# A four-layer graph network on one core: the expert buffer is cleared earlier, one-hot matrices are made by ScalarE, and a step's slot sums give one signal

## What is computed

```python
# every edge part with attention; h is a projection of the nodes
score = f(h[src], h[dst])                       # one per edge and head
m = segment_max(score, dst); e = exp(score - m[dst])
out = segment_sum(e * value[src], dst) / segment_sum(e, dst)
# layer 2's experts: two of eight per node
top_p, top_idx = top_k(softmax(x @ Wr + br), 2)
y_e = gelu(xn_e @ W1[e] + b1[e]) @ W2[e] + b2[e]
x = x + sum(weight * y[top_idx])
```

## Time and profile before

| what | us |
|---|---|
| median of 3 runs | 13737.19 |
| lowest and highest | 13736.53, 13757.31 |
| the profiled execution, its own time | 13846.6 |
| its span | 13844.9 |

### The profile page before, as it was taken

How to read it: one execution, slowest core, us unless ns; L and a number is a source line. 1 busy time by engine, 2 the same in 40 slices (tenths; PEclk the granted TensorE clock), 3 DMA queues, 4 the chain that set the end, 5 groups by cost and what they waited for, 6 DMA issues and landing times. The chain is left out here.

```text
span 13844.9 us, 108219 instructions
## 1 busy us (share of the span) xinstructions
PE 7534.6 (54%) x30838; PEld 6003.5 (43%) x30838; DVE 6330.2 (46%) x16971; ACT 1340.8 (10%) x3400; POOL 6032.2 (44%) x6195
## 2 busy tenths in 40 slices
PE   3333433346665455586777564545544936666535
PEld 2333333335554345554566433333433835555423
DVE  6555654558886422232112245656522134454454
ACT  0000000000000100011122010000011200010001
POOL 1666366046664066603666406656301036666000
PEclk9999999777777655587788786777776967777767
DMA  1111111046666011202333602212523323336000
GB/s 41 53 51 54 38 54 44 13 139 172 178 178 134 13 8 8 8 14 68 92 90 90 60 13 48 47 41 44 27 26 97 109 58 93 95 94 86 19 7 16
DMA packets 454853, 872.00 MB, mean 63 GB/s; under 512 B 172059, under 2 KB 267149, under 8 KB 453907
## 3 DMA queue, kind: packets, MB, share of 16 engines
q0 software_dynamic: 277568, 621.62, 21.4%
q1 hardware_dynamic: 176714, 243.62, 6.1%
HBM read 820.84 MB, written 52.88 MB: 63 GB/s over the span
## 5 line engine op out<-in xcount | busy, mean ns | idle before, releaser
L552 POOL DMA_INDIRECT ee_rows<-e_table,net_mr_data x1000 | 993.6, 994 | 1038.7 <-POOLq L1656 469.2
L552 POOL DMA_INDIRECT ge_rows<-g_table,net_mr_data x1000 | 959.0, 959 | 674.2 <-issue 241.7
L855 POOL DMA_INDIRECT ce_rows<-c_table,net_mr_data x1000 | 947.2, 947 | 511.6 <-issue 245.5
L387 POOL DMA_INDIRECT main_slots<-em_load,em_where x784 | 809.6, 1033 | 642.5 <-DVE em_where L362 395.6
L552 POOL DMA_INDIRECT ae_rows<-a_table,net_mr_data x752 | 722.5, 961 | 592.5 <-POOLq L1656 202.4
L589 PE MATMUL ee_part_ps<-ee_message,net_eye 125*125 125x256 f32 x2000 | 607.8, 471 | 523.6 <-issue 300.8
L552 POOL DMA_INDIRECT be_rows<-b_table,b_br_data x728 | 696.2, 956 | 434.7 <-issue 172.9
L589 PE MATMUL ge_part_ps<-ge_rows,net_eye 125*125 125x256 f32 x2000 | 624.8, 481 | 304.7 <-ACT ge_part L650 210.2
L346 PE MATMUL em_look_ps<-em_table,em_hot_tT 25*128 25x125 f32 x1568 | 366.9, 421 | 739.3 <-issue 655.3
L589 PEld LDWEIGHTS ee_part_ps<-ee_message,net_eye 125*125 125x125 f32 x2000 | 472.7, 241 | 639.0 <-issue 542.4
L387 POOL DMA_INDIRECT gat_slots<-eg_load,eg_where x512 | 531.7, 1039 | 381.5 <-DVE eg_where L362 217.1
(11 more groups left out here) (1004 smaller groups left out, 16859.0 us busy)
## 6 DMA issues: line engine op xcount, KB each, us to landing
em_key_row<-main_keys SPq DMA_DIRECT2D x98, 512.0 KB
f_w<-in_L_ffn_W_dram SPq DMA_DIRECT2D x40, 1024.0 KB, 5.1
eg_key_row<-gat_keys SPq DMA_DIRECT2D x64, 512.0 KB
ce_rows<-c_table,net_mr_data POOLq DMA_INDIRECT x1000
ee_rows<-e_table,net_mr_data POOLq DMA_INDIRECT x1000
ge_rows<-g_table,net_mr_data POOLq DMA_INDIRECT x1000
main_slots<-em_load,em_where POOLq DMA_INDIRECT x784
ae_rows<-a_table,net_mr_data POOLq DMA_INDIRECT x752
```

The source lines that it names most:

```text
L387: pool.indirect_dma_start(edge["slots"], bass.IndirectOffsetOnAxis(ap=where[:, c:c + 1], axis=0), load[:, c, :], None).then_inc(scattered, 16)
L552: pool.indirect_dma_start(rows[n][:, s, :], None, table, bass.IndirectOffsetOnAxis(ap=data[:, g, s, 0:1].bitcast(I32), axis=0)).then_inc(g ...
L855: pool.indirect_dma_start(rows[:, g % RING, s, :], None, table, bass.IndirectOffsetOnAxis(ap=data[:, g, s, 0:1].bitcast(I32), axis=0)).the ...
```

## The change

1. `sorted_in`, `sorted_out` and the semaphore `cleared` are made in `program`. Between the load of X and the first sort, VectorE clears a tile of 128 x 22 x 256 words, and the sync engine issues three DMAs of 2816 rows each from it to `sorted_in` (22 KiB a partition) and one to the last 256 rows of `sorted_out`. Behind the first sort stands a block in which the sync engine waits for them. The two DMAs in `layer2_experts` go; the clearing of A stays there.
2. In the attention passes the one-hot moves from VectorE to ScalarE, as |target - ramp| and then relu(1 - that), with a drain between, first in ScalarE's order of a step, for step i+4.
3. In the attention passes the 8 slot sums give one signal, after the last. GpSimd waits for it before a step's first gather alone; ScalarE's and VectorE's waits count steps. "ce" is not changed.

```diff
@@ edge_pass, gpsimd @@
                             if kind == "mix":
                                 pool.wait_ge(message_ready, g - RING + 1)
-                            else:
-                                pool.wait_ge(slot_summed, (g - RING) * SLOTS + s + 1)
+                            elif s == 0:
+                                pool.wait_ge(slot_summed, g - RING + 1)
@@ tensor, sum_slots @@
-                        pe.matmul(part_ps[0:NP, 0:VW], const["eye"][0:NP, 0:NP], values(g)[:, s, :], start=(s == 0), stop=(s == SLOTS - 1)).then_inc(slot_summed, 1)
+                        ins = pe.matmul(part_ps[0:NP, 0:VW], const["eye"][0:NP, 0:NP], values(g)[:, s, :], start=(s == 0), stop=(s == SLOTS - 1))
+                    ins.then_inc(slot_summed, 1)
@@ scalar @@
+                def one_hot(g):
+                    if g >= HOTS:
+                        act.wait_ge(totalled, g - HOTS + 1)
+                    act.activation(hot[0:NP, g % HOTS, :], const["ramp"][0:NP, 0:2 * NP], ACT.Abs, scale=-1.0, bias=edge["rel"][0:NP, g:g + 1])
+                    act.drain()
+                    act.activation(hot[0:NP, g % HOTS, :], hot[0:NP, g % HOTS, :], ACT.Relu, scale=-1.0, bias=const["ones"][0:NP, 0:1]).then_inc(hot_ready, 1)
...
-                    act.wait_ge(slot_summed, (g + 1) * SLOTS)
+                    act.wait_ge(slot_summed, g + 1)
...
-                for i in range(-3, G + 7):
+                for i in range(-4, G + 7):
+                    if 0 <= i + 4 < G:
+                        one_hot(i + 4)
@@ vector @@
-                def one_hot(g):
-                    if g >= HOTS:
-                        dve.wait_ge(totalled, g - HOTS + 1)
-                    dve.tensor_scalar(hot[0:NP, g % HOTS, :], const["ramp"][0:NP, 0:2 * NP], edge["rel"][0:NP, g:g + 1], None, ALU.is_equal).then_inc(hot_ready, 1)
...
-                            dve.wait_ge(slot_summed, (g - 1) * SLOTS)
+                            dve.wait_ge(slot_summed, g - 1)
...
-                    if 0 <= i + 4 < G:
-                        one_hot(i + 4)
@@ routed_rows @@
-                pool.wait_ge(cleared, 32)
+                pool.wait_ge(cleared, 64)
@@ layer2_experts @@
-            @block.sync
-            def _(sp):
-                sp.dma_start(sorted_in, I["zeros256"].to_broadcast([F_ROOM + 256, D])).then_inc(cleared, 16)
-                sp.dma_start(sorted_out[F_ROOM:F_ROOM + 256, :], I["zeros256"].to_broadcast([256, D])).then_inc(cleared, 16)
@@ program @@
-        sort_edges(nc, main, I["src"], I["dst"], I["edge_attr_2"], E_MAIN, const, "em", inv_deg)
...
+        with Scope(nc, "blank") as j:
+            share = (F_ROOM + 256) // 128 // 3
+            blank, made = j.sb("blank", [128, share, D]), j.sem("made")
+            with nc.Block() as block:
+                @block.vector
+                def _(dve):
+                    dve.memset(blank[:, :, :], 0.0).then_inc(made, 1)
+
+                @block.sync
+                def _(sp):
+                    sp.wait_ge(made, 1)
+                    for n in range(3):
+                        sp.dma_start(sorted_in[n * share * 128:(n + 1) * share * 128, :].rearrange("(p a) w -> p a w", p=128), blank[:, :, :]).then_inc(cleared, 16)
+                    sp.dma_start(sorted_out[F_ROOM:F_ROOM + 256, :].rearrange("(p a) w -> p a w", p=128), blank[:, 0:2, :]).then_inc(cleared, 16)
+            sort_edges(nc, main, I["src"], I["dst"], I["edge_attr_2"], E_MAIN, const, "em", inv_deg)
+            with nc.Block() as block:
+                @block.sync
+                def _(sp):
+                    sp.wait_ge(cleared, 64)
```

More of the change, by code:

```diff
@@ L2429, in _, with layer2_experts @@
                     dve.scalar_tensor_tensor(out=X[0:NP, t, :], in0=back[0:NP, n % RING, :], scalar=share[0:NP, t, c:c + 1], in1=X[0:NP, t, :], op0=ALU.mult, op1=ALU.add).then_inc(joined, 1)
-def layer2_experts(nc, I, X, const, lower):
+def layer2_experts(nc, I, X, const, lower, sorted_in, sorted_out, cleared):
     with Scope(nc, "f") as k:
@@ L2435, in layer2_experts @@
         w1, back = k.sb("w1", [128, 2, 2, 1024]), k.sb("back", [128, 8, D])
-        sorted_in = nc.dram_tensor("f_sorted_in", (F_ROOM + 256, D), F32, kind="Internal").ap()
-        sorted_out = nc.dram_tensor("f_sorted_out", (F_ROOM + 256, D), F32, kind="Internal").ap()
-        cleared, loaded1, loaded2 = k.own_sem("cleared"), [k.own_sem(f"loaded1_{n}") for n in range(2)], k.own_sem("loaded2")
+        loaded1, loaded2 = [k.own_sem(f"loaded1_{n}") for n in range(2)], k.own_sem("loaded2")
         slot, share, tile_expert = k.sb("slot", [128, T, 2], I32), k.sb("share", [128, T, 2]), k.sb("tile_expert", [1, F_TILES], I32)
@@ L2669, in program @@
         on_vector(nc, "x_in", lambda dve: None, loads=[(X[0:NP, :, :], table_rows(I["x"]))])
-        sort_edges(nc, main, I["src"], I["dst"], I["edge_attr_2"], E_MAIN, const, "em", inv_deg)
+        sorted_in = nc.dram_tensor("f_sorted_in", (F_ROOM + 256, D), F32, kind="Internal").ap()
+        sorted_out = nc.dram_tensor("f_sorted_out", (F_ROOM + 256, D), F32, kind="Internal").ap()
+        cleared = k.own_sem("cleared")
+        with Scope(nc, "blank") as j:
[16 more added lines that the diff above has]
+                    sp.wait_ge(cleared, 64)
         sort_edges(nc, gat, I["gat_src"], I["gat_dst"], None, E_GAT, const, "eg")
@@ L2674, in program @@
                   lambda: layer1_graph(nc, I, X, inv_deg, main, const), lambda: layer1_experts(nc, I, X, const, lower),
-                  lambda: layer2_graph(nc, I, X, main, const), lambda: layer2_experts(nc, I, X, const, lower),
+                  lambda: layer2_graph(nc, I, X, main, const), lambda: layer2_experts(nc, I, X, const, lower, sorted_in, sorted_out, cleared),
                   lambda: layer3_graph(nc, I, X, main, const), lambda: layer3_tokens(nc, I, X, const)]
```

## The result

The kernel after takes 13573.08 us, median of 4 runs (13552.31 to 13577.39), the kernel before 13745.99, median of 4 (13736.53 to 13757.31): a ratio of 0.9871 [0.9854, 0.9888], 173 us less [154, 201]. The forecast was 766 less. The profiled execution of after took 13552.31 us; that of before lay 0.8% over its median, so the two profiles are 294 us apart, and the runs' 173 is the number to explain.

What follows compares the result with a forecast made beforehand. The prediction took TensorE's slowly draining signals, which hold GpSimd's gathers, to bound the passes. It took 690 us (single signal) plus 76 (clearing), 766, from the median 13737: 12971 us. Its range was 12790 to 13430.

Steps and rivals of the forecast that it cites:

- What bounds the passes: Edge passes: GpSimd stands 1.5 to 2.2 us a step because TensorE's signals, not its work, arrive late.
- the doubt about modelled ends: TensorE's slot sums: ends of matmuls are modelled, so the sums themselves, not their signals, could be late.
- a queue of signals that drains slowly: TensorE's signals while GpSimd gathers: 11.5 a step drain at one a microsecond and hold GpSimd until they are through.
- The term of 690 us: ae, be, ee and ge: one signal for the slot sums saves 130, 128, 250 and 182 us, near the gathers' floor.
- The forecasts of 10.2 and 10.5: Microseconds a step after the change: 10.2 in be and ge, 10.5 in ee, near the gathers' floor.
- The 3.1 us later wait: GpSimd's gather into slot 0 waits for the last sum, some 3.1 us later; contained in the passes' forecast steps.
- The one-hot at nothing: Attention passes: ScalarE's two added operations, 1.2 us a step with the drain, are covered and cost nothing.
- The clearing: Moved from layer 2 to the start: 104 us saved, 28 us of delay before the first sort, net 76 less.
- Signals by the page's rule: Rival, chance 0.10: signals cost tens of nanoseconds, sums really end late, passes stay and 76 us go: 13660.
- Slow signals: Rival, chance 0.15: each signal stays slow, the step's chain limits, passes gain 230 to 345 us: 13320 to 13430.
- The coarse wait: Rival, chance 0.09: GpSimd waits for the last slot, costing 230 to 330 or 700 us, ae tightest: 13900 to 14350.
- Tables: Rival, chance 0.03: ScalarE changes tables between Abs or Relu and Exp, two 1.28 us loads a step: 14000 or so.

Runs made afterwards that it cites:

- e9: The kernel after, summing only slot 0 of the eight in the four attention passes, on a late chip: 13442.79 us, 0.9778 of before.
- e10: The kernel after, with plain loads by SyncE's queue in place of GpSimd's gathers in be and ge, on a late chip: 12533.44 us, one execution.
- e5: The kernel after, unaltered, on a punctual chip: 12637.45 us, 0.9984 of before.
- e7: The kernel before with its eight signals, but GpSimd waits at slot 0 for the eighth sum, punctual chip: 12707.84 us, 1.004 of before.
- e8: The kernel after, but ae keeps a signal and a wait for each slot, punctual chip: 12571.86 us, 0.9933 of before.
- e2: The kernel before with only the one-hot moved to ScalarE, punctual chip: 12686.43 us, 0.9997 of before.
- e6: The kernel before with the clearing and the one-hot moved, eight signals kept, punctual chip: 12568.58 us, 0.9931 of before.
- e1: The kernel before with only the clearing moved, punctual chip: 12611.30 us, 0.9938 of before.
- e18: The kernel before with only the clearing moved, late chip: 13748.03 us, 0.9929 of before.
- e16: The kernel before with only the one-hot moved to ScalarE, late chip: 13785.23 us, 0.9959 of before.
- e12: The kernel before with the clearing and the one-hot moved, eight signals kept, late chip: 13640.75 us, 0.992 of before.

## Why the prediction was wrong, point by point

- **What bounds the passes: half right.** TensorE's signals do come late and not its work; the doubt about modelled ends is answered by e9 and e10, and by e5, where signals stand 0.01 us behind the modelled ends. The step that failed is the next one, "a queue of signals that drains slowly", priced at one a microsecond because 11.5 signals stood beside a step of 11.6 us. That was a coincidence of two numbers, and the rows held a warning that I left out: ee sends 9.5 signals, the fewest, and had the longest step, 12.5 us. With 4.5 signals the lag and the step stayed. What sets the rate is GpSimd's gathers: in be 11.5 us for eight on a late chip, 10.0 on a punctual one, whatever the signals, the sums and the ring are. Why a late chip allows no more isn't shown.
- **The term of 690 us.** On a late chip the single signal gave 66, 41 of it in ae. On a punctual one be, ee and ge are at 10.0 to 10.3 before any change. The forecasts of 10.2 and 10.5 were thus right as floors and reached by a chip, not by the change.
- **The 3.1 us later wait.** I costed it, and called ae the pass with least slack. It is what the punctual chips show alone: 49 us by e7 and 66 by e5 against e8, 0.4 to 0.5 us a step in ae. On late chips its cost isn't seen, and why the single signal gains in ae there wasn't tried.
- **The one-hot at nothing.** ScalarE's two operations took 0.504 and 0.503 us, 1.0 us a step beside the forecast 1.2, and are hidden. No table load but one a pass came. On punctual chips it is nothing in sum (6 us), with 17 to 22 us won in ae, where I had placed its use, and 9 to 11 lost in ee (e2 and e6 against e1). On late ones it gives 57 [35, 79], mostly in ee, which I had not seen: I had given VectorE's 0.34 us a use in ae alone. The cause within ee is not shown.
- **The clearing: right.** Layer 2: 102 us where I had 100.5, and 2.9 for the weights where I had 3.5 (the wait for them is 3.69 in place of 6.59). Start: 23.6 later in place of 28. Net 76 forecast, 81 and 85 [68, 127] measured for the clearing alone (e1, e18). The 18.5 us that the sort's scatters took less in the profile of after are no part of it, as e16 and e18 show.
- **The sum.** Late chips: 85 + 66 + 57 = 208, against 173 [154, 201] for all three; punctual: 81 + 6 - 53 = 34, against 22 [9, 32]. The part that is short on late chips is the pair of e12, 105 [82, 137], where e16 and e18 add up to 142. Each of these is known to 20 or 30 us only, and they stand on three chips, so whether the parts add up isn't settled closer than that.
- **The rivals.** "Signals by the page's rule" (13660: passes stay, 76 go) came nearest and had 0.10; its reason, that the sums' real ends are late, is wrong. The rule itself, 26 ns a signal, an estimate of 85 us (the Trainium skill, "TensorE: Matmul & The Clock Gate", "The cost: per-tile semaphore tail"), is not borne out where signals are punctual: e8 leaves out seven signals in 341 steps against e6 and is 3 us slower. Taken off the median with the 76, those 85 would give 13576, the measured time but for 3 us; that would have been luck, as on late chips the single signal's gain lies in ae and none in be and ge. "Slow signals" named the chain, but priced it as part of the 690. The coarse wait was right in place on punctual chips, in ae, and too dear in price: 230 us or more against 49. Tables: no.
- **The range** missed because both cases that it took in shared one premise, that fewer signals shorten the passes by a third or more of 690 us.

## What to carry to other kernels

When a signal arrives late, ask what else is running at that moment before counting signals: here the release came after GpSimd's stop, and one kernel without gathers (e10) would have told it at once. A floor read from busy time (eight gathers, 10 us) is reached on one chip and not on another: compare a stage that the change leaves alone, as ce. And before one signal replaces several, look at who waits for the first of them: with a ring of 4 it cost 49 to 66 us, with 5 next to nothing.

## What was not expected of the hardware

- Two kinds of chip: the same kernel takes 12660 to 12690 us on two and 13740 to 13840 on the others, all of it where GpSimd issues indirect DMAs. Of one kernel, e18 is 1141 us longer than e1, and its two sorts' scatters and five passes are 1183 longer; of the earlier trace rows against e1, be 913 against 1056 us, ge 1282 against 1457, the main sort's scatters 1040 (below) against 1202 [from the rows of L387 above].

```profile
L387 POOL DMA_INDIRECT main_slots<-em_load,em_where x784: 952/958/1784, 316.5 to 1356.4; - x196
```

- On a late chip TensorE's signals wait while GpSimd gathers, up to 10.9 us in the row above, and come together within 0.23 us some 3 us after the last gather. With plain loads the copies come after 0.04 us, and on a punctual chip the signals come after 0.01 us though GpSimd gathers without a stand. What in the chip they share with the gathers stays open.
- The releasers that the views name for such waits on late chips (a load of another stage, "remote") were not the true ones in any of these rows. A likely reason is that late chips record fewer events: the trace of after has 30,474 semaphore events of landed DMAs, that of e5, the same kernel on a punctual chip, has 108,339. Whether the recording has a part in the delay itself was not tested.
- Seven eighths of the sums left out made after 130 us faster on a late chip (13443 against 13573) though be and ge barely moved, 9 and 15 us. The windows show 59 us of it in ee and 20 in ae. As ee takes 1495 to 1529 us in the late runs that leave its code as in after, part of this may be spread.
